# Signalling every gathered block behind the next block's second gather, in the second graph layer of a two-layer GNN with routed FFNs

## What the reference computes

```python
x = x + gru_gnn(layernorm(x), ...)      # layer 0, graph part: segment sum of h[src] + relation vectors, then a GRU
x = x + ffn_top2_of_4(layernorm(x), ...)  # layer 0, FFN part
# layer 1, graph part (the stage that is changed here)
xt = layernorm(x) @ W.T + b
x = x + segment_sum(xt[src], dst) / (degree + 1)
# layer 1, FFN part: top 2 of 8 experts, 256 -> 1024 -> 256
x = x + ffn_top2_of_8(layernorm(x), ...)
```

## Time and profile before

| what | value |
|---|---|
| median of 3 runs | 3546.89 us (3544.86 to 3551.88) |
| span of the profiled execution, first to last instruction | 3473.6 us |
| median less span | 73.3 us |
| busy share of the span: PE, DVE, ACT, POOL | 68%, 44%, 24%, 59% |
| layer 1's gathers on POOL | 784, from 1514.0 to 2681.7 us of the span |

### The profile page before, as it was taken

How to read it: one execution, slowest core, us unless ns; L and a number is a source line. 1 busy time by engine, 2 the same in 40 slices (tenths; PEclk the granted TensorE clock), 3 DMA queues, 4 the chain that set the end, 5 groups by cost and what they waited for, 6 DMA issues and landing times. The chain is left out here.

```text
span 3473.6 us, 47355 instructions
## 1 busy us (share of the span) xinstructions
PE 2350.7 (68%) x11708; PEld 1592.8 (46%) x11709; DVE 1527.9 (44%) x4042; ACT 835.8 (24%) x1644; POOL 2057.1 (59%) x2208
## 2 busy tenths in 40 slices
PE   1488898899667564446666555444433699999996
PEld 1255555555334231223333222212111599899896
DVE  7455555555443242144645533333120455555553
ACT  2233333333222120021111000000000244444442
POOL 0364545556666666446666666666665466766764
PEclk6599999999878776557776666655555799999998
DMA  5222222223322332223333333333333433323324
GB/s 166 85 85 66 75 71 77 81 84 90 91 85 82 89 89 79 67 85 93 99 96 99 94 94 94 93 90 97 89 94 100 134 67 65 65 41 67 66 40 104
DMA packets 166676, 297.70 MB, mean 86 GB/s; under 512 B 51015, under 2 KB 110256, under 8 KB 166352
## 3 DMA queue, kind: packets, MB, share of 16 engines
q0 software_dynamic: 100192, 234.80, 25.9%
q1 hardware_dynamic: 41620, 39.61, 3.7%
q10 hardware_dynamic: 24732, 21.86, 2.0%
HBM read 255.39 MB, written 47.14 MB: 87 GB/s over the span
## 5 line engine op out<-in xcount | busy, mean ns | idle before, releaser
L755 POOL DMA_INDIRECT rows<-table,srcT x1568 | 1545.4, 986 | 965.6 <-issue 434.7
L821 PE MATMUL bank<-rows,onehot 128*128 x1952 | 674.1, 487 | 747.2 <-POOLq L743 695.7
L821 PEld LDWEIGHTS bank<-rows,onehot 128*128 x1952 | 217.9, 112 | 1159.1 <-issue 1031.4
L781 DVE SCALAR_TENSOR_TENSOR onehot<-iota_row,tbase,dstT 128x512 f16 x488 | 366.4, 753 | 633.0 <-PE bank L821 265.2
L1916 ACT ACTIVATE hid<-bank,b 128x256 f32<-128x256 f32 x432 | 181.8, 472 | 368.7 <-PE bank L1868 368.7
L1866 PE MATMUL bank<-xe_high,W_high 128*128 128x256 f32 x864 | 251.5, 291 | 27.0 <-DVE xe_low L1945 26.8
L1866 PE MATMUL bank<-W_high,hid_high 128*128 128x256 f32 x864 | 249.9, 289 | 0.0
L1867 PE MATMUL bank<-xe_low,W_high 128*128 128x256 f32 x864 | 249.6, 289 | 0.0
L1868 PE MATMUL bank<-xe_high,W_low 128*128 128x256 f32 x864 | 249.1, 288 | 0.0
L1868 PE MATMUL bank<-W_high,hid_low 128*128 128x256 f32 x864 | 245.0, 284 | 0.0
L1867 PE MATMUL bank<-W_low,hid_high 128*128 128x256 f32 x864 | 245.0, 284 | 0.0
(11 more groups left out here) (349 smaller groups left out, 3928.3 us busy)
## 6 DMA issues: line engine op xcount, KB each, us to landing
rows<-table,srcT POOLq DMA_INDIRECT x1568, 2.8
W<-in_L_ffn_W_dram SPq DMA_DIRECT2D x14, 1024.0 KB
x_res<-in_x_dram SPq DMA_DIRECT2D x1, 6144.0 KB, 23.1
table<-part ACTq DMA_DIRECT2D x11, 512.0 KB, 3.5
normal<-xn ACTq DMA_DIRECT2D x11, 512.0 KB, 3.3
totals<-x_res SPq DMA_DIRECT2D x11, 512.0 KB, 6.8
table<-part SPq DMA_DIRECT2D x6, 512.0 KB, 2.9
table<-part_b SPq DMA_DIRECT2D x6, 512.0 KB, 2.9
```

Of the source, the lines that this page charges most:

```text
L755: nc.gpsimd.indirect_dma_start(out=rows[:, k % (M * U), 0:ROW], out_offset=None, in_=q.table, in_offset=bass.IndirectOffsetOnAxis(srcT[:, ...
L781: last = nc.vector.scalar_tensor_tensor(onehot[:, ds(slot, U), :], iota_row[:, :].unsqueeze(1).to_broadcast([P, U, P]), base, dstT[:, ds(k ...
L821: last = nc.tensor.matmul(acc[:, 0:ROW], hots[:, ds(hot0 + s * P, P)], ring_rows[:, ds(row0 + s * ROW, ROW)], start=False, stop=False, ski ...
```

## The change

The second argument of layer 1's call becomes 196. Then `i % run > 0` holds for every block but block 0, and `i % run == run - 1` only for the last block, which was signalled there before too.

```diff
@@ -1622,7 +1622,7 @@
                                channel_multiplier=0).then_inc(R["cols_ready"], 1)
                 nc.gpsimd.iota(to_list[:, :], pattern=[[0, LCOLS // SUB], [1, SUB]], base=NPAD,
                                channel_multiplier=SUB).then_inc(R["spares_ready"], 1)
-                pool_chunks(pool, q2, 3)
+                pool_chunks(pool, q2, BLOCKS)
```

## The result

The changed kernel was slower: 3571.3 us (median of 5 runs, 3543.5 to 3594.3) against 3544.9 us (3524.7 to 3551.9) for before in the same series, a ratio of 1.009 with a 95% interval of 1.0053 to 1.0127. The forecast was 3400 us. The traced execution took 3543.5 us with a span of 3541.9 us, so only 1.6 us lie outside the span. It is the fastest of the five, 27.8 us under their median: the trace shows where the gain went, and nothing shows where the slower runs lose more.

A forecast was written before the change was run, and what follows sets the result against it. POOL's gathers were taken to bound layer 1. Removing 153.2 us of waits, with 2.0 and 3.9 us added back, saves 147.3 us from 3546.9: forecast 3400 us, range 3391 to 3417 us.

The forecast's parts named there:

- What the change removes: Layer 1's gathers: 65 long waits for landings, 172.75 us, shrink to 0.30 us each, so 153.2 us go.
- What it adds: Layer 1: 2.0 us for landings late at the moved waits, 3.9 us for gathers lengthened by DVE work beside them.
- Does PE keep up?: Layer 1: a replay with PE's work kept fixed put PE at most 5.6 us behind POOL's signals, so POOL isn't held.
- PE or DVE becomes the bound: Rival, first part of layer 1: POOL gains nothing or less there, 3445 us, partial case 3420 to 3445; chance 4%.
- The 73.3 us around it: Whole kernel: time taken to lie outside the span, added to the 3326.3 us span to give 3399.6 us.
- The shared port: Rival, layer 1: gathers lengthen by all DVE work that lay in the waits, 95.7 us saved, 3451 us; chance 2%.
- Landings: Rival, layer 1: landings get late once the queue never drains; chance of a loss 1%, of 3417 to 3445 us 4%.
- The gain was not given back: Rival, behind layer 1: something else sets the engines' meeting or the expert stage runs longer, 3547 us; chance 1%.

The follow-up runs named there:

- e14: The changed kernel itself, run again beside the unchanged kernel on a chip without late instructions: 3326.8 us against 3477.3, ratio 0.956.
- e1: The unchanged kernel, traced for a second look; span 3531.8 us or 3525.0 us (two such looks), timed at 3518.2 us on that chip.
- e2: The unchanged kernel once more, the other of two such looks; spans 3531.8 and 3525.0 us, timed at 3518.2 us on that chip.
- e4: Unchanged kernel, but layer 1 stops for a landing behind every second block, 98 waits in place of 65: 83.6 us above the unchanged kernel.
- e8: Unchanged kernel plus 200 copies of 512 KB from HBM to HBM on SP's queue during layer 1: ratio 1.0235.
- e3: Unchanged kernel, but layer 1 stops for a landing behind every block, 196 waits in place of 65: 308.7 us above the unchanged kernel.
- e5: Changed kernel, but each layer 1 gather fetches 512 B per row in place of 1 KB: ratio 1.0091.
- e7: Changed kernel plus an added POOL operation (0.34 us as it ran) behind each block of layer 1: 5.21 us for a block that nothing held.
- e9: Changed kernel with one gather per block of layer 1 in place of four: stage took 705.6 us from first gather to expert stage.
- run = 6: Unchanged kernel, but layer 1 stops for a landing behind every sixth block, 33 stops in place of 65: 73.9 us faster, ratio 0.9792, later 0.9798.
- the short stop: Unchanged kernel, but layer 1's wait for each third block's landing stands behind the next block's first gather: 78.5 us faster, ratio 0.9774, later 0.9775.

## Why the prediction was wrong

**What the change removes: right.** The 153.2 us of waits for landings went in every trace without the stops: idle time put down to the DMA is 4.0 us in after and 11.4 in e14. **What it adds: right in size.** Where instructions come in time, the stage took 1021.5 us, 2 us over the sum, and the gain was 150.6 us for 147.3.

**The step that failed** is "Does PE keep up?", with its words "PE's work between two of its 130 waits kept as it is". That work is not fixed. It was read from an execution without a single late instruction, and on the chip that timed the kernel PE's and DVE's instructions come late in stretches where POOL has no longer break. There the 65 stops did a second work that no row shows: after each of them PE had at least six gathers' time without late instructions (e1, e2, e4, e8). Without them PE alone has 334 late instructions, 234 us in all, 330.3 us of idle time before its gathered matmuls are put down to "issue", POOL fills the ring and is held for 161.0 us, and the 153.2 us are spent again. The rival that came nearest was the first, "PE or DVE becomes the bound"; it had the right place, `free` with a full ring, but 4% and a price of 20 to 45 us, limited to the first part of the stage. After's stage is held by PE to its end.

**A second step was wrong and would have warned.** "The 73.3 us around it" took the difference between the median and the span for time outside the instructions. Time and span of the same execution differ by 1.6 us here. The other 71.7 us were the sign that the traced execution and the timed ones ran under different conditions: where before has late instructions (e1, e2), its span is 51 to 58 us longer, 44 to 52 of it in layer 0, for the same program. What the timed runs of before had beyond that is in no trace. What stands ahead of the prediction makes the same mistake about these 73.3 us.

**The other rivals.** The shared port cost little: gathers were busy 776.1 us in e14 for 771.4 before, 4.7 us (forecast 3.9). Landings stayed in time: the median is 2.8 us in e14, as before. The gain was not given back behind the last gather: the tail is 37.9 us in e14 and 38.5 before; in after, where PE is late to the end, it is 44.0.

**What stays open.** Why some chips show late instructions and others don't, and whether it is the chip at all or the hour: no chip was seen both ways, the first three series have them and the last four don't, and the trace of before, the earliest, has none although before took 3544.9 us beside after. Whether a stop must let all gathers land, or a stand-still of POOL at a written place does; how the loss lies between 12 gathers per run and no stop, on such a chip. The runs meant for these last two met no late instructions. Layer 0's loss isn't accounted for either: e1 has some 22 late instructions each on PE and DVE there, 15 us on each engine, and the layer's gathers take 52 us more. Where they occur at all, the stops between POOL's gathers decide their number: that is shown by count and place (e1, e2, e3, e4 on one chip, e5, e7, e8, e9 on another), with the bytes excluded (e5). By which path the gathers bring them about is not shown.

No version beats both kernels on every chip that was seen. Where before takes about 3480 us, after is the best (3327). Where it takes 3518 us or more, before was better than after and than e4, and run = 6 and the short stop, which gain 2.0 to 2.3% on the other chips, were not timed.

## What to carry to other kernels

Compare the traced execution's own time with the timed runs before building a sum on it; a difference of 2% is a finding, not an overhead. A replay that keeps another engine's work fixed holds only for the conditions of that trace: ask what else a wait gives besides what it waits for, and give a chance to its absence slowing the others. Where an engine's idle time stands under "issue" with single instructions evenly apart, look at the register instructions between them before blaming a semaphore.

## What the runs showed of the hardware

- PE, DVE and, rarely, POOL can fall to one instruction per 0.7 us, register and branch instructions as well as matmuls, for some 35 us at a stretch (2687 to 2722 us in the trace of after). Later passes of a window's loop are hit as well as the first: three blocks of one window begin at 2687.34, 2699.99 and 2712.59 us, 12.6 us apart, where POOL needs 5.0 us for a block.
- It is there or not by the series: it is in the trace of after and in all eight traces of the first two groups of experiments, in layer 0 at least, and in none of the ten traces that followed, nor in that of before. Where it is there, it goes with back-to-back indirect gathers of 1.25 us each (334 late instructions on PE) and not with their bytes (295 with half of them).
- A stop that waits for a landing costs 2.36 us in POOL's queue, and 130 more of them cost 308.7 us in the kernel: 2.37 us each.
